# GATv2 pass: edge scores as one-column products and a new order of TensorE and VectorE; GAT pass: maxima and weights read in PSUM

## The reference, cut to what matters

```python
# layer 0 (GAT, H = 8 heads of F = 16)
e = leaky_relu(a_s[src] + a_d[dst], 0.2)
m = segment_max(e, dst)
p = exp(e - m[dst])
alpha = p / (segment_sum(p, dst)[dst] + 1e-16)
out = segment_sum(alpha[:, :, None] * xp[src], dst)
...
# layer 3 (GATv2, one head)
h = x_l[src] + x_r[dst]
h = where(h >= 0, h, 0.2 * h)
e = h @ att
e_max = segment_max(e, dst)
alpha = exp(e - e_max[dst])
alpha = alpha / (segment_sum(alpha, dst)[dst] + 1e-16)
out = relu(segment_sum(alpha[:, None] * x_l[src], dst) + bias)
```

## Time and profile before

| | us |
|---|---|
| three runs, median (lowest to highest) | 5962.01 (5955.12 to 5962.85) |
| the profiled execution, its own time | 5946.32 |
| its span | 5944.5 |
| GAT pass, window 235 to 1462 | 1227 |
| graph convolution, window 1601 to 2665 | 1064 |
| third pass, window 2845 to 4150 | 1305 |
| GATv2 pass, window 4725 to 5912 | 1187 |

### The profile page before, as it was taken

One profiled execution on the slowest core, in us unless ns is written; L12 is line 12 of the kernel. 1 busy time (PEld: TensorE's weight loads), 2 busy tenths in 40 slices (PEclk: granted clock), 3 DMA queues, 4 the chain that ended last, 5 costly groups with the idle time before them and its releaser, 6 DMA issues. The chain is left out here.

```text
span 5944.5 us, 95091 instructions
## 1 busy us (share of the span) xinstructions
PE 3804.6 (64%) x24005; PEld 3232.3 (54%) x24006; DVE 4148.1 (70%) x8912; ACT 1470.4 (25%) x3477; POOL 3529.3 (59%) x3528
## 2 busy tenths in 40 slices
PE   6366666665233333334688888887494188888886
PEld 5355555554233333324577777777364166666664
DVE  7599999999633333335899999999425266666666
ACT  0233333332000000001233333333111133333332
POOL 1477777774377777762566666664121266766663
PEclk5555555565655556566899999999697589989888
DMA  1233333332122222210222222222000933323322
GB/s 52 56 72 74 74 75 75 75 75 47 34 52 52 52 52 52 52 45 25 80 64 64 64 64 64 64 64 60 14 1 21 32 71 71 71 70 72 70 68 62
DMA packets 331427, 341.81 MB, mean 57 GB/s; under 512 B 186836, under 2 KB 233031, under 8 KB 331332
## 3 DMA queue, kind: packets, MB, share of 16 engines
q0 software_dynamic: 106832, 223.07, 16.4%
q1 hardware_dynamic: 224500, 117.67, 9.8%
HBM read 319.62 MB, written 21.66 MB: 57 GB/s over the span
## 5 line engine op out<-in xcount | busy, mean ns | idle before, releaser
L800 POOL DMA_INDIRECT e_G<-dr_tab,src_idx x832 | 941.5, 1132 | 272.5 <-issue 252.3
L800 POOL DMA_INDIRECT m_G<-dr_tab,src_idx x832 | 795.3, 956 | 490.5 <-PE m_OUT L1805 247.9
L800 POOL DMA_INDIRECT v_G<-dr_tab,src_idx x832 | 811.4, 975 | 448.2 <-issue 224.5
L800 POOL DMA_INDIRECT s_G<-dr_tab,src_idx x832 | 785.2, 944 | 275.3 <-issue 266.1
L1631 PE MATMUL s_OUT<-s_G,s_S 128*128 128x129 f32 x1664 | 390.0, 427 | 733.6 <-DMA s_G<-dr_tab,src_idx 733.6
L1631 PEld LDWEIGHTS s_OUT<-s_G,s_S 128*128 128x128 f32 x1664 | 361.9, 330 | 761.6 <-DMA s_G<-dr_tab,src_idx 678.1
L1604 DVE TENSOR_TENSOR ACC<-ACC,s_OUT 128x129 f32 x832 | 241.5, 290 | 680.6 <-PE s_OUT L1631 576.9
L1735 DVE TENSOR_TENSOR ACC<-ACC,m_OUT 128x512 f32 x832 | 564.5, 678 | 4.1 <-PE m_OUT L1805 3.6
L1804 PE MATMUL m_OUT<-m_XB,m_SE 128*128 128x256 f32 x1664 | 497.4, 381 | 0.0
L1803 PE MATMUL m_OUT<-m_G,m_S 128*128 128x128 f32 x1664 | 360.8, 299 | 196.4 <-DVE m_SE L1743 141.0
L1177 PE MATMUL e_OUT<-e_RH,e_S 128*128 128x145 f32 x1664 | 442.3, 457 | 11.5 <-DVE ACC L987 5.6
(11 more groups left out here) (346 smaller groups left out, 8514.0 us busy)
## 6 DMA issues: line engine op xcount, KB each, us to landing
e_LR<-dr_row_loc SPq DMA_DIRECT2D x104, 256.0 KB, 3.4
m_MS<-dr_row_start SPq DMA_DIRECT2D x104, 256.0 KB, 3.4
v_LR<-dr_row_loc SPq DMA_DIRECT2D x104, 256.0 KB, 3.4
e_G<-dr_tab,src_idx POOLq DMA_INDIRECT x832
s_G<-dr_tab,src_idx POOLq DMA_INDIRECT x832
m_G<-dr_tab,src_idx POOLq DMA_INDIRECT x832
v_G<-dr_tab,src_idx POOLq DMA_INDIRECT x832
dr_tab<-XPA SPq DMA_DIRECT2D x7, 476.0 KB, 3.1
```

Of the source, the lines that this page charges most:

```text
L800: pool.indirect_dma_start(out=out, out_offset=None, in_=table, in_offset=bass.IndirectOffsetOnAxis(ap=g["src_idx"][:, step:step + 1], axis ...
```

## The change

In the GATv2 pass the scores are made otherwise. `edge_scores` takes a step's `v_LZ` as weights and streams the single column `att_of`; eight products (two matmuls each in f32) give eight columns of 128 edges. VectorE adds the gathered linear part (`columns_out`, into `v_cols`) and TensorE turns that 128 x 8 into the 8 x 128 scores. Both engines' programs are written in another order. `destinations` and `turn` of the first half run a group further ahead, `sums` of a group move behind the next group's scores, in two pieces, and `node_slots_ahead` moves behind all of the group's additions. The factors go to `v_NX` beside the weights, and ScalarE copies both at once.

In the GAT pass the forward scan writes its result over `e_ET` in PSUM and the backward scan reads it there; the last column is kept by a small copy (`e_last`), and the turn of the maxima waits for it. `e_ST` is made by ScalarE in two operations (`node_slots`: Square into `e_SQ`, then Relu). The exponential is copied by ScalarE to PSUM (`e_PP`), where VectorE's product reads it. The flag is computed once for all groups (`e_has`), and `ACC` has 144 columns in place of 145.

```diff
@@ SoftmaxParts
+    def node_slots(self, act, k, i, b, read):
+        c = b % 2
+        wait_alone(act, self.locrow_in[c], 16 * (2 * i + b // 2 + 1), self.stood)
+        if not isinstance(k, int) or k > 0:
+            wait_alone(act, self.st_done, k, self.stood)
+        self.nc.scalar.activation(self.SQ[:], self.LR[:, c, :], ACT.Square, bias=self.g["iota_col"][:], scale=-1.0).then_inc(self.sq_done, 1)
+        wait_alone(act, self.sq_done, k + 1, self.stood)
+        wait_alone(act, read, k - 1, self.stood)
+        self.nc.scalar.activation(self.ST[:, c, :], self.SQ[:], ACT.Relu, bias=self.g["ones"][:, 0:1], scale=-1.0).then_inc(self.st_done, 1)
...
-        V.tensor_tensor_scan(out=FW[:, p, :], data0=self.MS[:, p, :], data1=self.scores[:],
-                             initial=FW[:, 1 - p, SLOTS - 1:SLOTS], op0=ALU.add, op1=ALU.max).then_inc(self.maxima_step, 1)
+        V.tensor_tensor_scan(out=self.ET[:], data0=self.MS[:, p, :], data1=self.ET[:],
+                             initial=last[:, 1 - p:2 - p], op0=ALU.add, op1=ALU.max).then_inc(self.maxima_step, 1)
...
+        V.tensor_tensor_scan(out=CM[:, ::-1], data0=self.ME[:, p, ::-1], data1=self.ET[:, ::-1],
+                             initial=-BIG, op0=ALU.add, op1=ALU.max).then_inc(self.cm_step, 1)
+        V.tensor_copy(last[:, p:p + 1], self.ET[:, SLOTS - 1:SLOTS]).then_inc(self.cm_done, 1)
...
@@ gat_pass
+                    wait_alone(act, exp_done, k + 1, parts.stood)
+                    nc.scalar.copy(weight, RH[:, b % 2, :, D:D + heads]).then_inc(parts.p_done, 1)
...
-                                    RH[:, b % 2, steps, D:D + heads].unsqueeze(3).to_broadcast([P, GROUP // 4, heads, hd]),
+                                    weight[:, steps, :].unsqueeze(3).to_broadcast([P, GROUP // 4, heads, hd]),
...
@@ gatv2_pass, VectorE
                 def body(k, i, b):
                     if not is_first(k):
                         tiles = tiles_of(k - 1)
                     maxima_in_steps(k, i, b)
+                    if not is_last(k):
+                        larger(k + 1, 0)
+                    over_steps(k, i, b)
                     onehots(k, b)
+                    maxima(k, b)
+                    if not is_first(k):
+                        add(k - 1, b + 1, tiles, range(0, 3))
+                    if not is_last(k):
+                        larger(k + 1, 1)
+                    if not is_first(k):
+                        add(k - 1, b + 1, tiles, range(3, 6))
+                    factors_of_nodes(k, b)
+                    if not is_first(k):
+                        add(k - 1, b + 1, tiles, range(6, GROUP))
                     if not (isinstance(k, int) and k >= GROUPS - 2):
                         node_slots_ahead(i, b)
...
+                        columns_out(k + 1, (b + 1) % 4)
...
@@ gatv2_pass, TensorE
+                def edge_scores(k):
                     pe.wait_ge(lz_done, 2 * k + 2)
+                    wait(pe, dif_done, k)
                     for s in range(GROUP):
+                        ins = nc.tensor.matmul(columns[:, s:s + 1], LZ[:, s * P:(s + 1) * P], att_of[:], start=True, stop=True)
+                    ins.then_inc(columns_done, 1)
...
+                    step_scores(k)
+                    if not is_first(k):
+                        sums(k - 1, b + 1, range(0, 3))
                     last_of_steps(k)
                     if not is_last(k):
                         destinations(k + 1, b + 1, tiles, 1)
                         turn(*nxt, 1)
                     before_steps(k, b)
+                    if not is_first(k):
+                        sums(k - 1, b + 1, range(3, GROUP))
+                    if not (isinstance(k, int) and k >= GROUPS - 2):
+                        tiles = tiles_of(k + 2)
+                        turn(*then, 0)
                     turn_weights(k)
                     if not is_last(k):
+                        edge_scores(k + 1)
+                    if not (isinstance(k, int) and k >= GROUPS - 2):
+                        destinations(k + 2, b, tiles, 0)
```

More of the change, by code:

```diff
@@ L884, in body @@
             wait(sp, self.st_done, k - 1)
+            wait(sp, self.lf_done, k - 1)
             locrow(k, c)
@@ L1086, in _ @@
                 parts.prepare(dve)
+                c.then(V.tensor_scalar(has[:], g["loc_end"][:], 0.0, None, ALU.is_ge))
                 def differences(k, b):
@@ L1249, in gatv2_pass @@
         ROWS = ctx.enter_context(nc.psum_tensor("v_ROWS", [P, 512], F32))
-        nodes, weights = NODES[:, 0:P], NX[:, 0:GROUP]
-        scores, factors = ROWS[0:GROUP, 0:P], ROWS[:, P:P + GROUP]
+        nodes = NODES[:, 0:P]
+        weights, factors = NX[:, 0:GROUP], NX[:, GROUP:2 * GROUP]
+        scores, columns = ROWS[0:GROUP, 0:P], ROWS[:, P:P + GROUP]
         last_row, before = ROWS[0:1, 160:160 + GROUP], ROWS[0:GROUP, 192:193]
@@ L1338, in weighted_rows @@
                 def weighted_rows(k, b):
+                    wait_alone(act, r_done, k, stood)
                     wait_alone(act, weights_done, k + 1, stood)
-                    nc.scalar.copy(PW[:], weights).then_inc(pw_done, 1)
+                    nc.scalar.copy(PW[:], NX[:, 0:2 * GROUP]).then_inc(pw_done, 1)
                     wait_alone(act, pw_done, k + 1, stood)
@@ L1360, in _ @@
                 V.memset(state[:, 0:1], -BIG).then_inc(start, 1)
[L1361 removed]
                 V.tensor_copy(nodes, g["iota_row"][:]).then_inc(start, 1)
[L1363 to L1366 removed]
+                V.tensor_scalar(att_of[:], att, 1.0 - SLOPE, None, ALU.mult).then_inc(start, 1)
                 for j in range(PARTS):
@@ L1518, in turn_weights, with sums @@
                 def turn_weights(k):
-                    pe.wait_ge(fac_done, k + 1)
-                    pe.wait_ge(dif_done, k + 1)
-                    nc.tensor.matmul(factors, fac[:].to_broadcast([GROUP, P]), g["eye"][0:GROUP, 0:GROUP],
-                                     start=True, stop=True).then_inc(factors_done, 1)
                     if not is_last(k):
                         pe.wait_ge(nxs_done, 2 * k + 4)
+                    pe.wait_ge(fac_done, k + 1)
+                    nc.tensor.matmul(factors, fac[:].to_broadcast([GROUP, P]), g["eye"][0:GROUP, 0:GROUP], start=True, stop=True)
                     wait_alone(pe, pr_done, k + 1, stood)
                     nc.tensor.transpose(weights, PR[:], g["eye"][0:GROUP, 0:GROUP]).then_inc(weights_done, 1)
-                def sums(k, b):
-                    pe.wait_ge(s_done, k + 1)
-                    for s in range(GROUP):
+                def sums(k, b, steps):
+                    if steps[0] == 0:
+                        pe.wait_ge(s_done, k + 1)
+                    for s in steps:
                         if s % 3 == 0:
@@ L1537, in _ @@
                 tiles = tiles_of(0)
-                pe.wait_ge(start, 7)
+                pe.wait_ge(start, 6)
                 for h in range(2):
@@ L1554, in body @@
                     before_steps(k, b)
+                    if not is_first(k):
+                        sums(k - 1, b + 1, range(3, GROUP))
+                    if not (isinstance(k, int) and k >= GROUPS - 2):
+                        tiles = tiles_of(k + 2)
+                        turn(*then, 0)
                     turn_weights(k)
                     if not is_last(k):
-                        step_scores(k + 1, (b + 1) % 4)
-                    sums(k, b)
+                        edge_scores(k + 1)
+                    if not (isinstance(k, int) and k >= GROUPS - 2):
+                        destinations(k + 2, b, tiles, 0)
                 in_groups_of_four(pe, body)
+                sums(GROUPS - 1, GROUPS - 1, range(GROUP))
         sem.clear()
```

108 lines of the change are left out of this document (52 added, 56 removed).

## The result

The changed kernel takes 5996.1 us (median of 5 runs, 5991.8 to 6000.6), the kernel before 5962.0 beside it (5935.3 to 5967.3). The ratio is 1.0067, 95% interval 1.0045 to 1.009: slower, by 34 us in the medians, where 83 were forecast. By the profiled executions it is 5990.0 - 5944.5 = 45.5 us, where the prediction's own sum was 86.

A forecast was written before the change was run, and what follows sets the result against it. It took TensorE to bound the GATv2 pass and VectorE the GAT pass. The profiled 5946.3 us plus 76 (GATv2) plus 10 (GAT) gave 6032, with 15.7 for the median 6048, rounded to 6045; range 5935 to 6125.

The forecast's parts named there:

- T: GATv2 pass: the start of `v_running` in a group, from which the forecast laid out the group's times.
- Step 5: GATv2 pass, TensorE: sixteen one-column matmuls take 2.25 us at full clock, 4.5 at half; at full clock hidden by VectorE.
- the flag: GAT pass, VectorE: the comparison of `loc_end` with zero goes from each group, saving 0.18 us a group.
- the four products reading PSUM: GAT pass, VectorE: reading weights in PSUM costs 0.04 us for each product, taken as 0.1 us a group.
- the backward scan and the turn that waits for `e_last`: GAT pass: the scan reading PSUM costs 0.04 us more a group, the turn waiting for the small copy 0.09.
- ScalarE's second operation: GAT pass: a second pass of ScalarE ahead of the first product costs 0.03 us a group.
- 2 us more at the start: GAT pass, start: ScalarE makes the first two `e_ST` one after another, costing 2 us once.
- the gather that the scan no longer holds back: GAT pass: GpSimd is freed 1.6 us a group, which nobody waits for, so no gain was counted.
- The rival that had GpSimd as the bound of the whole pass: GAT pass: freeing GpSimd gives up to 156 us, net 5880 us with the other pass's loss; chance 0.04.
- The order works as written: GATv2 pass: `v_ST` is no wait, GpSimd bounds at 9.9 us a group, kernel about 5840 us; chance 0.16.
- The full clock holds: GATv2 pass: full clock but the wait for `v_ST` stays, 11.4 us a group, kernel 5986 us; chance 0.18.
- the clock stays at half for most of the loop: GATv2 pass: TensorE mostly at half clock, 13.0 us a group, kernel 6151 us; chance 0.10.

The follow-up runs named there:

- early_st: Changed kernel with `v_ST` made ahead of the maxima instead of last, on a chip where the kernel before takes 7337.7 us: 7565.9 us, ratio 1.031.
- gat_only2: Changed kernel with the GATv2 pass of the kernel before: 5913.7 us against 5959.8 for the kernel before, ratio 0.9934.
- scan_sbuf3: Changed kernel with the GAT pass's forward scan writing to SBUF, so the backward scan reads two SBUF tensors again: 6008.8 us, ratio to before 1.0102.
- v2_only2: Kernel before with the GATv2 pass of the changed kernel, its GAT pass left as it was: 6030.2 us, ratio 1.0122.
- early_st2: Changed kernel with VectorE making `v_ST` right behind the one-hots, ahead of the maxima, instead of last in the group: 5782.2 us, ratio to before 0.9714.

## Why the prediction was right in one half and wrong in the other

**GATv2 pass: right**, in size and in mechanism. With T = 5202.20 in the group shown: from the turn of the last column to `v_CM` 2.55 us (2.65 taken), `v_CM` at T + 3.9 (3.5), from there to the end of `v_ST` 5.38 (5.93), `v_ST` ready at T + 9.3 (9.4), from there to the next `v_running` 2.88 (2.5), the group 12.15, its mean 12.07 (12.0 taken). The one-column products end at T + 8.5 (8.7) and are no bound. The errors of single terms are up to 0.55 us and cancel, which is luck as far as 12.0 against 12.07 goes: the half clock, forecast for the sums' first steps and the turns, is there (granted clock 0.50 from T to T + 3.8, 1.00 under the one-column products) and `v_CM` comes 0.4 later than taken; VectorE's pieces behind it are 0.55 shorter than added up. Step 5 took 2.25 us for the sixteen products at full clock and the trace has 1.95; at half the clock (granted 0.50), on the slow chip, `early_st` has 3.58. So such a matmul costs 0.12 us, and their weight loads alone take 1.86 of the 1.95: the column costs next to nothing. The price was near the upper end, and mattered not at all.

**The clock: right.** 0.71, with 0.75 expected. The Trainium skill, "TensorE: Matmul & The Clock Gate", section "What's actually happening", has half speed as the state from which activity lifts the clock. The rows agree as far as they go: 0.71 with TensorE standing twice a group, 0.82 when `v_ST` came earlier and nothing else was changed, 0.90 with the old code in `gat_only2`.

**The GAT pass: the step that failed.** +0.08 us a group and 10 us in all were forecast, -0.22 a group in the middle of the pass and -32 us in all were measured. That is 42 us of error; the GATv2 pass (+7) and the stretch between the passes (-6) nearly cancel in the remaining difference from 86 to 45.5. Term by term: the flag -0.18, measured -0.205; the four products reading PSUM **+0.10, measured -0.04**; the backward scan and the turn that waits for `e_last` **+0.04 and +0.09, measured together +0.03** from the start of the scan to `e_DIF` (the scan itself went from 2.278 to 2.275 us); ScalarE's second operation +0.03, measured nothing; 2 us more at the start, measured 2 less. Each unknown small cost was taken above zero, and nearly all were zero or below. The scan's price is instructive: 2.32 against 2.28 was put down to PSUM, but the forward scan differs from the backward one in other ways, and turned to PSUM the backward scan did not become longer. The wait for the turned maxima grew, and `e_ST`'s removal brought nothing, both as forecast.

**A second term was put at nothing:** the gather that the scan no longer holds back, "which nobody waits for". The earlier trace rows begins at 300 us, and its four waits are the last of the start. In the middle of the pass the reading is right, and so is the one that the held-back gather takes up whatever GpSimd has to spare: `scan_sbuf3` has the long gather back and a period of 11.26 us against 11.25. But in the first groups VectorE does wait for gathers, 9.6 us from 261 to 370 us, and most of that is gone (8 us of the 32). And in other executions of the old code, as in `v2_only2`, gathers hold VectorE up all through the pass, 20 us in all. The medians fit with that: `gat_only2` is 46 us under the kernel before, where the starts in the profiled executions give 32. The sum added the same 15.7 us to the profile's time for both kernels, and the changed one has 4.3. The rival that had GpSimd as the bound of the whole pass, at 0.04, did not come. That VectorE's instructions with two SBUF inputs contend with GpSimd (the Trainium skill, "GPSIMD Engine Reference", section "1. Specifications") is shown here for the backward scan: one edit brings the 2.4 us gather back.

**The rivals.** "The order works as written" named the point from which it decides, `v_ST` ready before T + 8.7. The change misses it by 0.6 us. `early_st2` passes it, with 10.03 us a group where 9 to 10 and the gathers' 9.9 were worked out. "The full clock holds" and "the clock stays at half for most of the loop" both did not come. The range, 5935 to 6125, holds the time. The change was 34 us where 83 were forecast, and it is the GAT pass that makes the difference.

## What to carry to other kernels

When an order is rewritten around one chain, look at what else stands in the queue of the engine that is waited for: here 0.47 us of VectorE's work, made last instead of early, cost 2 us a group through a wait on TensorE, matmuls at the pace of its sequencer, a bared register load and a falling clock. An engine without a pause is not a bound by that alone: its busy time and issue always add up to the period. Compare its instructions with their unhindered length, and see who waits for it, from the pass's first group on, since a window that begins later hides the start. Don't give every unknown small cost a positive price: let the measured neighbours set a mean and keep the sign open.
